# Second of two query chunks five steps behind the first, and seven smaller moves in the plan of a four-layer kernel

## The reference, cut to what matters

```
x = LN(x + linear_attention(x))      # 4 x 2048 tokens, D = 256, 16 heads, 64 random features
x = LN(x + fp4_ffn(x))               # 704 hidden; input, weights, hidden values quantized in blocks of 16
x = LN(x + attention(x))             # batch 4, 16 heads of 16, latent K and V (64), rotary by head index
x = LN(x + moe(x))                   # top 2 of 8 experts, capacity 160, two groups of 4096 tokens

linear_attention: q_phi = (exp(q.orf/dk^.25 - |q|^2/(2 sqrt dk)) + 1e-6)/8, likewise k_phi
                  out = (q_phi @ (k_phi^T v)) / (q_phi . sum k_phi);  out @ Wo^T + bo
```

## Time and profile before

| | us |
|---|---|
| median of the runs | 4567.32 |
| the profiled execution | 4571.13 |
| its span, first to last instruction | 4569.3 |
| TensorE busy | 4315.6 (94%) |
| VectorE busy | 3491.5 (76%) |
| ScalarE busy | 2811.9 (62%) |
| POOL busy | 978.9 (21%) |
| mean granted TensorE clock | 0.976 of full |

### The profile page before, as it was taken

How to read it: one execution, slowest core, us unless ns; L and a number is a source line. 1 busy time by engine, 2 the same in 40 slices (tenths; PEclk the granted TensorE clock), 3 DMA queues, 4 the chain that set the end, 5 groups by cost and what they waited for, 6 DMA issues and landing times.

```text
span 4569.3 us, 66262 instructions
## 1 busy us (share of the span) xinstructions
PE 4315.6 (94%) x25817; PEld 1642.9 (36%) x25820; DVE 3491.5 (76%) x3858; ACT 2811.9 (62%) x5305; POOL 978.9 (21%) x957
## 2 busy tenths in 40 slices
PE   8999789999989999999999999999999899999895
PEld 5555446656632222222222222222222232222385
DVE  3555789878887788887778888778888988888242
ACT  4333323333337788887777777777777667787621
POOL 3333433544222100001211111211111010100213
PEclk9999989999989999999999999999999999999997
DMA  3102000122123312113241221323221222122232
GB/s 111 35 29 66 19 11 14 51 81 73 69 73 117 97 69 69 43 68 102 91 138 54 85 77 59 131 80 106 81 70 71 60 67 70 62 71 81 77 113 52
DMA packets 230277, 330.49 MB, mean 72 GB/s; under 512 B 36870, under 2 KB 171464, under 8 KB 227912
## 3 DMA queue, kind: packets, MB, share of 16 engines
q1 hardware_dynamic: 227084, 318.40, 21.2%
q0 software_dynamic: 2880, 7.87, 0.9%
HBM read 218.71 MB, written 98.04 MB: 69 GB/s over the span
## 4 chain that ended last, share of the span: by engine, by line
PE 68%; DVE 11%; DMA 3%; POOL 2%; issue 2%; ACT 1%; SPq 1%; POOLq 0%; DVEq 0%; another core or an unknown queue 0%; ACTq 0%
PE ps L754 66%; DVE mx L1597 4%; PE ps L757 2%; DMA pk<-Ob 1%; DVE stat L1424 1%; DVE hn L1418 1%; DMA x2d<-eb 1%; DVE qs L1492 0%; DVE hn L1576 0%; DMA rd<-pk 0%; DVE hn L1571 0%; DMA KS<-kd 0%; SPq L2072 0%; DVE eb L1435 0%; DMA QS<-mrow 0%
## 5 line engine op out<-in xcount | busy, mean ns | idle before, releaser
L1597 DVE TENSOR_REDUCE mx<-ps 128x1 f32<-128x1024 f32 x2048 | 2407.6, 1220 | 421.8 <-PE ps L754 418.4
L1346 ACT ACTIVATE Pb<-ps 128x512 f32<-128x512 f32 x4096 | 2202.6, 597 | 518.8 <-PE ps L754 514.6
L754 PE MATMUL ps<-QS,KS 98*128 98x512 bf16 x4096 | 1249.8, 386 | 16.4 <-ACT Pb L1346 7.4
L754 PE MATMUL ps<-Pb,VA 128*32 128x512 f32 x8192 | 1094.2, 606 | 0.1
L754 PE MATMUL ps<-KM,QM 64*128 64x512 bf16 x4096 | 658.5, 388 | 52.2 <-DVE mx L1597 50.3
L754 PEld LDWEIGHTS ps<-QS,KS 98*128 98x128 bf16 x4096 | 260.2, 97 | 1086.2 <-ACT Pb L1346 902.0
L754 PEld LDWEIGHTS ps<-KM,QM 64*128 64x128 bf16 x4096 | 180.0, 93 | 607.3 <-issue 349.1
L754 PEld LDWEIGHTS ps<-Pb,VA 128*32 128x32 f32 x8192 | 161.2, 108 | 400.5 <-issue 399.5
L1901 POOL CAST mrow<-mres 16x128 bf16<-16x128 f32 x64 | 18.5, 288 | 1269.2 <-ACT mres L1182 1269.2
L754 PE MATMUL ps<-wdT,hT 128*128 128x256 f32 (+1 forms) x768 | 193.5, 394 | 15.8 <-DVE X L1582 14.3
L1504 DVE RECIPROCAL rB<-ps 128x512 f32<-128x512 f32 x28 | 94.0, 3358 | 106.8 <-PE ps L754 106.7
(11 more groups left out here) (235 smaller groups left out, 4340.0 us busy)
## 6 DMA issues: line engine op xcount, KB each, us to landing
QM<-qd SPq DMA_DIRECT2D x128, 256.0 KB
KM<-kd SPq DMA_DIRECT2D x128, 256.0 KB
qd<-parts SPq DMA_DIRECT2D x96, 256.0 KB, 2.7
kd<-parts SPq DMA_DIRECT2D x96, 256.0 KB, 2.8
QS<-qd SPq DMA_DIRECT2D x64, 384.0 KB
KS<-kd SPq DMA_DIRECT2D x64, 384.0 KB
vdr<-vst SPq DMA_DIRECT2D x64, 256.0 KB, 2.5
den<-rd SPq DMA_DIRECT2D x64, 256.0 KB
```

The source lines that it names most:

```text
L754: return eng.matmul(out, a, b, start=start, stop=stop, skip_group_check=skip)
L1346: eng.activation(Pb[(u - 1) % 9], o, ACT.Exp, bias=0.0, scale=0.25).then_inc(act_A, 1)
L1597: eng.tensor_reduce(mx4[qc % 2][:, 4 * i + q, h:h + 1], o, AX, ALU.max).then_inc(dve_D, 1)
```

## The change

Eight edits, all of them in the order of the list: no instruction of any engine is added or removed.

1. The stream of chunks 13 and 15 starts five entries behind that of 12 and 14.
2. In batch 3 `res` stands beside `pq` (1, 1) in place of (0, 1).
3. `inputs_order` waits four entries, spaces its steps, and joins `xb` in pairs.
4. `prep_order` puts two `pv` behind `ps` of q and two behind `ps` of k, in place of four at the end.
5. In the bridge a background unit follows two of three maxima.
6. `fetch` of head 3 for group 13 stands at step 57 of group 12 in place of 62.
7. `we` 0, 1, 2 stand at steps 8, 24, 40 of group 15 in place of all at 0; `we` 3 and the ten gathers `gx` at step 56 in place of 52.
8. At the end three scatters of the first half stand ahead of the second half's `yp` and two behind its `yn`.

```diff
+WEIGHTS = {8: 0, 24: 1, 40: 2}
...
-        yield [("pq", C, 0, 1), ("res", C)]
+        yield [("pq", C, 0, 1)] + ([("res", C)] if b < 3 else [])
         yield [("pq", C, 1, 0)]
         yield [("num", C, 0)]
-        yield [("pq", C, 1, 1)]
+        yield [("pq", C, 1, 1)] + ([("res", C)] if b == 3 else [])
...
 def inputs_order(G):
-    for step in (("qx", G), ("xa", G), ("xb", G, 0), ("xb", G, 1), ("xb", G, 2), ("xb", G, 3)):
-        yield [step]
+    yield from [[]] * 4
+    yield [("qx", G)]
+    yield [("xa", G)]
+    yield []
+    yield []
+    yield []
+    yield [("xb", G, 0), ("xb", G, 1)]
+    yield [("xb", G, 2), ("xb", G, 3)]
...
-        for w in "qk":
+        for i, w in enumerate("qk"):
             for ht in range(2):
                 yield [("pp", b, c, w, ht)]
             yield [("ps", b, c, w)]
-        for j in range(4):
-            yield [("pv", b, c, j)]
+            for j in range(2):
+                yield [("pv", b, c, 2 * i + j)]
...
-        yield [("ys", g, 0), ("yp", g, 1), ("yn", g, 1), ("ys", g, 1)]
+        yield [("ys", g, 0, 0, 3), ("yp", g, 1), ("yn", g, 1), ("ys", g, 0, 3, 5), ("ys", g, 1)]
...
-    together(plan, queries_order(3, (0, 2), 11), queries_order(3, (1, 3), None), chain(inputs_order(0), inputs_order(1)))
+    together(plan, queries_order(3, (0, 2), 11), chain([[]] * 5, queries_order(3, (1, 3), None)), chain(inputs_order(0), inputs_order(1)))
...
-        if made % 2 == 0 and made > EARLY + 2 and ("mx", 0, 0) not in plan:
+        if made % 3 and made > EARLY + 2 and ("mx", 0, 0) not in plan:
...
-            if n == 15:
-                plan += [("we", e) for e in range(3)]
-        if n + 1 < 16 and st % 16 == FETCH:
+        if n == 15 and st in WEIGHTS:
+            plan.append(("we", WEIGHTS[st]))
+
+        if n + 1 < 16 and st % 16 == (9 if (n, st // 16) == (12, 3) else FETCH):
...
-        if step == 64 * 15 + 52:
+        if step == 64 * 15 + 56:
...
-        def ys(g, f):
+        def ys(g, f, a=0, z=5):
...
-            for b in range(5 * f, 5 * f + 5):
+            for b in range(5 * f + a, 5 * f + z):
```

## The result

| | before | after |
|---|---|---|
| median, 20 runs each on one chip, us | 4565.49 (4551.51 to 4577.20) | 4554.60 (4543.33 to 4562.79) |
| the profiled execution, us | 4571.13 | 4551.25 |
| its span, us | 4569.3 | 4549.4 |
| mean granted TensorE clock | 0.976 | 0.979 |

The ratio after to before is 0.9974, 95% interval 0.9965 to 0.9984. The change made the kernel 11 us faster. The forecast was 41 us (4530).

The account below looks back on a forecast made before the run. Each stage was priced by its full engine: TensorE in the FFN and second attention, VectorE in the last chunks. Terms -3 - 16 - 4 - 8 - 7.5 - 2.3 = -40.8 us from 4571.1 gave 4530; range 4508 to 4557.

Parts of the forecast that it names:

- Last chunks: Last four query chunks of the first attention: stagger, bias and input moves together give -3 us, bounds -26 and +23.
- the prediction's other value, 20: Last chunks: VectorE's stretch beside POOL's long operations stays 20 us if every meeting is kept, instead of falling to about 10.
- Rival (a): Last chunks: the stagger is paid in steps, five at 4.7 us, +23; total 4556 us; chance 0.12.
- prep_order: FFN of layer 0: reordered preparation removes TensorE's three stops behind vst and pres; -16 us, bounds -19 and 0.
- the 18.6 us: FFN: TensorE's waits of 5.17, 4.24 and 2.16 us plus 7 us of work lost to the lower clock.
- The bridge: Into the second attention: four more background units cost +3.3 us there, save 7.3 later; -4, bounds -8 and +3.
- fetch (13, 3): Second attention, start of group 13: earlier load ends TensorE's wait for KS and low clock; -8 us, bounds -8.5 and -5.
- Weights: Group 15: spreading the experts' weights lets pk land sooner, ending TensorE's wait and low clock; -7.5 us, bounds -8 and +3.
- step 56 in place of 52: Last steps of group 15: moving we 3 and the ten gathers gains 0 us, bounds -3 and +3.
- End: Final scatters: with three issued first, POOL no longer waits for normalized rows; -2.3 us, bounds -2.6 and 0.
- Rivals (b) to (e): In order: FFN stops move, 4546, chance 0.13; SP falls behind, 4624, 0.03; more gained, 4510, 0.12; nothing visible, 4563, 0.05.
- signs of being wrong: Last-chunks stage over 125 us, new ScalarE waits for vst or pres, or VectorE waits for eb after steps 24 and 40.

Follow-up runs that it names:

- e3: The kernel before with edits 1 to 3 alone; median 4579.47 us, ratio 1.0027 to the kernel before.
- e9: The changed kernel with edit 1 (stagger) alone undone; median 4535.63 us, ratio 0.9904 to the kernel before.
- e4: The changed kernel with each group's third and fourth input quantization on POOL one entry later, behind the last scaling of chunks 13 and 15; one run, 4558.53 us.
- the ledger's kernels: The kernel after and six experiment kernels, one profile each, whose stretches between stage boundaries were compared with the kernel before.
- e5: The kernel before with edits 1, 2, 4, 6, 7, 8 (input quantizations placed as before); one run, 4541.03 us (before 4555.21).
- e12: The kernel before with edit 5 alone; one run, 4594.47 us (before 4581.02).
- e8: The kernel before with edits 4 to 8 and one background unit more ahead of the first S; one run, 4528.40 us (before 4555.21).
- e10: The kernel before with edits 2 to 8 and one background unit more among the ten maxima, as in e8; median 4534.95 us, ratio 0.9891.
- e2: The kernel before with edits 4, 6, 7, 8 alone; median 4528.15 us, ratio 0.9910 to the kernel before.
- e6: The kernel before with edits 2, 3, 4, 6, 7, 8 (new input places, no stagger); one run, 4518.70 us (before 4555.21).
- e13: Second run of the kernel before with edits 4 to 8 alone, to recount clock dips behind router units; profile 4534.87 us.

## Why the prediction was wrong, step by step

**Last chunks: the failed step.** The value -3 was taken between bounds of -26 and +23; it is +10.9 (e3: +12.8). Both terms of it fail in size. The stretch was to fall from 13.0 + 6.9 = 19.9 to about 10. The squares still average 1058 ns for 1090 and the normalizing 773 for 760, so by the same prices the stretch is 12.0 + 7.2 = 19.2; the prediction's other value, 20 if every meeting is kept, is what came. The waiting before the additions was to grow by about 7 from 6.1; it grew by 12.1 to 18.2. These two, -0.7 and +12.1, are 11.4 of the stage's 12.5. The working laid the new order out by hand with each engine's durations and saw o of chunk 12 meet a projection of 13, but put too little on it: VectorE and TensorE take both streams in one queue each, so an addition waits for a product behind the other stream's projection, and the product for an aT that VectorE makes between the other stream's operations. That the stagger does it is shown by e9 (18.2 us of waiting against 6.2 with edit 1 alone changed); how the two queues divide it between them is read from the timeline and from e4's exchange of waits, and not shown by itself.

Rival (a), five steps more at 4.7 us, +23, comes near edit 1 alone: +18.7 of stage, +20.3 to the first tile. Its mechanism is not borne out, since two steps cost 0.5 of stage where its price gives 9. That the measured time stands beside its 4556 is luck: the prediction's 4530 is missed by 13.9 in the last chunks and by 12.3 in and behind the bridge, which (a) knew nothing of. The gain of 6 to 8 us by edits 2 and 3 was not priced by itself; the prediction took three edits as one sum.

**prep_order.** -16 forecast, -13.0 to -16.4 measured in the ledger's kernels with it, -10.2 in e5 (where the clock was low for longer, as said above), -0.8 and +0.8 in two without. Right, and as described: waits of TensorE in the FFN are these and no others, where the earlier trace rows had vst and pres (total us, times, longest).

```profile
PE ps L765 <- DVE X L1593: 19.8, 16, 4.3
PE ps L765 <- DVE mx L1608: 2.3, 2, 1.2
PE ps L768 <- DVE hn L1589: 2.2, 1, 2.2
```

Over the tiles TensorE's idle time fell from 26.7 to 17.0 us and the time at the clock's lower level from 27.3 to 13.7: both terms of the 18.6 us are there, the waits for X having grown by some 3.

**The bridge: the other failed step.** -4 forecast (bounds -8 and +3), +8.3 measured (3.4 + 4.9; e12 alone +12.1). The +3.3 in the bridge was right (3.2 to 5.1 in the ledger's kernels and e8), to a tenth by luck. The -7.3 behind it did not come: the shift moved later units against things that stay put. Two stops, a timeline of TensorE at each (start, us, form, idle before):

```profile
1478.50 0.71 PE L765 MATMUL ps<-QS,KS 98*128 98x512 bf16 x2 [1.87 <-DMA QS<-mrow]
...
1536.53 0.72 PE L765 MATMUL ps<-QS,KS 98*128 98x512 bf16 x2 [4.35 <-DMA KS<-kd]
```

Behind each the clock is at its lower level for some us (0.62 in 1480 to 1483 and in 1538 to 1541), and a router unit at 1400 has one too. With two steps' shift the part behind the bridge gives 4.6 to 5.3 of the 7.3 us, and the whole of bridge and groups 0 and 1 is -0.2 (e8, e10): no loss, but no gain either, and e2, without edit 5, has -0.7 there. No run shows the 4 us. The prediction looked at what stands around the moved step in SP's queue for the edits that name such a step (fetch, weights), but for this one it took four units fewer behind the bridge as pure gain, and did not ask what the later units of the batch, all eight steps earlier now, stand in front of. The bound of +3 was too tight for that reason.

**fetch (13, 3).** -8 forecast, -7.4 to -9.7 in the ledger (-6.2 in e6, -10.0 in e5). Right: between 3756 and 3766 TensorE is busy 8.88 of 10 us at clock 1.00, where the earlier trace rows had 1.62 of 7.

**Weights.** -7.5 forecast, -7.9 to -8.0. Right:

```profile
4139.00:4147.00 8.00, 8.00 (x50) 1.75 (x50) 7.33 (x9) 6.64 (x13) 1.27 (x1) 1.00 0.11 36
```

The queue moves 36 GB/s there for the 425 of the earlier trace rows, and the 4.16 us of the earlier trace rows and the low clock behind them are gone. VectorE's reciprocal of pk starts 7.7 us after SP's issue, without idle time before it, for 13.1. For step 56 in place of 52, 0 was forecast; -2.1 is there, but e3 without edit 7 has -2.0, so 0 stands.

**End.** -2.3 forecast, -2.2. VectorE's wait for rstd is 1.74 us, against 4.31, and POOL scatters without the pause of the earlier trace rows. The timeline of VectorE, then of POOL:

```profile
4535.17 1.79 DVE L1446 TENSOR_SCALAR xr<-xr,mv,rstd 128x256 f32<-128x256 f32 x5 [1.74 <-POOL rstd L1840]
```

```profile
4533.94 1.20 POOL L1840 TENSOR_TENSOR rstd<-vpe,nhalf 128x5 f32<-128x5 f32 x1
4535.33 1.22 POOL L1952 DMA_INDIRECT out_y<-xr,tabs  x1 [0.20 <-issue]
4536.86 0.97 POOL L1952 DMA_INDIRECT out_y<-xr,tabs  x1 [0.30 <-issue]
```

**The sum.** From -40.8: the last chunks +13.9, the bridge and after +12.3, groups 2 to 12 +5.4 (three router units with a dip, some 4.6, the rest small), and 1.5 less from the four right steps (which brought more) make -10.7; -0.9 ahead of the chunks, -2.1 in the last steps and -6.2 in the experts, none of them by an edit, lead to the -19.9 of the profiles. Without the stall of before's execution that is -12.3, and the medians say -10.9. Rivals (b) to (e) did not happen. Of its signs of being wrong, the stage of the last chunks came closest, 124.8 us for "over 125".

## What to carry to other kernels

Two streams of one chain in step with each other are not waste by themselves: here, with one queue for each engine, in step was 20 us faster than five entries apart and 4 faster than two. An offset must be timed alone, apart from what is moved with it. When an edit changes how many background units have been used up by some point, list what the later ones now stand in front of in every queue (here: a store that waits for POOL, one step ahead of the maxima and the next loads); two steps decided over 10 us. Price edits one at a time even where they act in one stage, and where edits shift many later units, set the bound by the waits that they could meet: the bridge's +3 left out a meeting that the list shows.

## What the runs showed of the hardware that was not expected

TensorE's granted clock fell without any idle time. In the kernel after, a timeline of TensorE around a router unit (16 matmuls of 8 columns), and windows of the same microseconds, with TensorE busy throughout:

```profile
1399.32 1.06 PE L765 MATMUL ps<-Pb,VA 128*32 128x512 f32 x8
1400.31 1.95 PE L765 MATMUL ps<-wrc,x2T 128*128 128x8 f32 x16
...
1404.23 1.94 PE L765 MATMUL ps<-Pb,VA 128*32 128x512 f32 x8
```

```profile
1399.00:1402.00 3.00, 3.00 (x25) 1.85 (x24) 2.03 (x2) 1.29 (x3) 0.00 (x0) 1.00 0.08 14
1402.00:1405.00 3.00, 3.00 (x16) 0.89 (x19) 1.92 (x2) 2.49 (x6) 0.98 (x3) 0.80 0.22 81
1405.00:1408.00 3.00, 3.00 (x16) 0.38 (x8) 0.90 (x2) 1.09 (x3) 1.26 (x1) 0.64 0.01 1
```

The V product behind the unit takes 1.94 us where the one before took 1.06: the lower of the clock's two levels, 1.2 GHz for 2.4. It costs 1.5 us a time, up to 12 us an execution in these groups, and the same kernel had eight and none. That is large enough to be a good part of the spread of this kernel's runs (20 us within 20 runs; which of them had dips is not on record), and a reason to take a difference of a few us in long, fully busy stretches as no one's doing until a second profile has it. The Trainium skill (TensorE: Matmul & The Clock Gate, "What's actually happening") has the chip's monitor running freely, not restarted by a kernel; the two executions of one kernel agree with that. The Trainium skill (the same page, "HAM oscillation — how this bites in real kernels") tells of clock lost behind waits for DMA. The stop at 1536 (4.35 us, clock 0.62 behind it) agrees with that; here the clock also falls behind narrow matmuls with TensorE busy 9.00 us of 9.00, so a gap is not needed.

Left open: what makes the experts' stall come and go (between the 12th and 13th result 7.6 us in before and 4.4 to 6.7 in e9 to e12, which share a chip; in e10 8.0 more before the sixth; in e13 nowhere), and whether splitting the router units ends the dips.
